# Moving the latent products of a pair of heads behind the transposes of the same slot

## The chip, the cores and the metric

The kernel runs on one core of a Trainium2 chip. The metric is the device time of one execution in microseconds (us), the median over the runs of a kernel. All times in the profile come from one profiled execution.

## The reference

Four sequences of 512 rows of width 512 pass through half a feed-forward step with low-rank adapters, an attention with a compressed key and value, and the feed-forward step again. The change lies in the attention alone:

```python
x = x + 0.5 * _L0_ffn_ref(_layernorm(x), ...)
x = x + _L0_attn_ref(_layernorm(x), ...)
x = x + 0.5 * _L0_ffn_ref(_layernorm(x), ...)

# _L0_attn_ref, H = 32 heads, latent width KVL = 64
q_lat = jnp.einsum('bhsd,hdr->bhsr', q_nope, wuk)
scores = jnp.einsum('bhsr,btr->bhst', q_lat, c_kv) + jnp.einsum('bhsd,btd->bhst', q_rope, k_rope[:, 0])
scores = scores / jnp.sqrt(jnp.float32(DN + DR))
scores = jnp.where(causal, scores, jnp.finfo(scores.dtype).min)
probs = jax.nn.softmax(scores, axis=-1)
out_lat = jnp.einsum('bhst,btr->bhsr', probs, c_kv)      # the latent products
out = jnp.einsum('bhsr,hdr->bhsd', out_lat, wuv)
return out.transpose(0, 2, 1, 3).reshape(b, s, H * DV) @ w_out
```

## The kernel before

The program is written engine by engine: each engine has its own queue with the order written out by hand, and semaphores tie them together. After an opening that loads and folds the weights, a loop runs three times and its body stands once more behind it for the fourth sequence: `attend(b)` (the attention of one sequence) and `steps(b, ...)` (the feed-forward steps and the projections for the next). In the loop a wait is on a value that is computed into a register first; in the copy for the fourth sequence waits are on constants.

`attend` goes over 16 pairs of heads. A pair has five units (`UNITS`), each one 128x512 bank of scores or less: the rows of a head with four key blocks (units 0 and 1, one for each head), with three and one (units 2 and 3), and the two-block rows of both heads (unit 4). So there are 80 slots, `u = 5*p + k`, and each engine walks through them with `work(g, u)`. In slot u:

- TensorE (PE) computes the scores of unit u (L849 to L851), in slots k = 0 and 2 the query products of the next pair (L834), the transposes of the probabilities of unit u - 3 (`T_LAG`; L870, four of 128x128), and in slots k = 1 and 4 an output product (L911, six matmuls) of heads two pairs or more back, from the fourth pair on. In slot k = 3 (`PV_SLOT`), the fourth of a pair, it also computes the latent products of the pair before, `pv(b, g, p - 1)` (L885, 20 entries in the trace).
- VectorE (DVE) adds the mask and takes the row minimum of the negated scores (L1490), the reciprocal of the row sums of the unit before (L1445), the rotary products of the queries (L1436 to L1438), the low part of the latent output (L1497), the copies of transposed units k = 1 and 3 (L369), and the output's addition to x (L1449).
- ScalarE (ACT) takes the exponentials with their row sums (L1120), the high parts of queries (L1091) and latent output (L1102), and the copies of transposed units k = 0, 2 and 4 out of PSUM into `probT` (L367).
- GpSimd (POOL) sums the rotary halves (L496), takes the low part of queries (L501) and multiplies the probabilities by the reciprocal sums (L576), one or two instructions for each unit.

What the slot k = 3 waits for. The transposes of unit 0 (`transpose_probs(b, g, u - 3)`) wait for POOL's multiplication of that unit (`prob_scaled`) and for the copy that frees their bank (`probT_by_dve`, the copy of unit 3 of the pair before). `pv` of the pair before waits for all copies of that pair: the last is ACT's copy of its unit 4 (`probT_by_act`), whose transposes stand in slot k = 2 and whose place on ACT is behind the exponentials of slot k = 2. It waits further for the two halves of the latent output before it (`oT_hi_set`, `oT_lo_set`). `probT` has one buffer, so the copies of the new pair wait for `pv_done`: ACT's copy of unit 0 stands in its slot k = 3 and waits for `pv_done` and for the transposes of unit 0. The scores of slot k = 4 follow on PE.

Of the kernel before, what the change touches and what calls it, by code (L numbers as in the profile page):

```python
# [72 lines left out]
T_LAG = 3  # L73
# [34 lines left out]
def build(nc, hidden, w_q_down, w_q_up_nope, w_q_up_rope, w_kv_down, w_k_rope, w_uk, w_uv, w_out,  # L108
          W_base, b_base, lora_A, lora_B, router_W, router_b, domain_prior, active,
          rope_cos, rope_sin, rope_cosT, rope_sinT, out):  # L110
    with ExitStack() as ctx:
# [206 lines left out]
        def attention(slot_work, tail):  # L318

            for g in range(BODIES):  # L320
                for u in range(BODY + (tail if g == BODIES - 1 else 0)):
                    slot_work(g, u)

        def known(g, u, least):

            return not isinstance(g, int) or BODY * g + u >= least

        def within(g, u, most):

            return not isinstance(g, int) or BODY * g + u <= most  # L330
# [5 lines left out]
        def output_rows(u):  # L336

            p, k = u // UNITS, u % UNITS
            slots = OUT_SLOT if u < BODY else OUT_SLOT_TAIL
            return 2 * ((p + 1) % 2) + slots[k] if k in slots else None  # L340
# [33 lines left out]
        def q_index(b, n, head):  # L374

            return 34 * b + 2 + 2 * n + head

        SLOTS = UNITS * PAIRS
        LAST_PAIR = PAIRS - 1

        with nc.Block() as block:
# [208 lines left out]
            def _(pe):  # L590
# [234 lines left out]
                def q_products(m, n, head, cols=slice(0, S), bank_free=True):  # L825

                    if bank_free:
                        pe.wait_ge(q_rot_set, m - 1)
                    hi, lo, rest = (w[:, 2 * n + head, :]
                                    for w in (wq1_hi, wq1_lo, wq2))  # L830
                    parts = ((hi, cq_hi[:, 0, cols]), (lo, cq_hi[:, 0, cols]), (hi, cq_lo[:, 0, cols]),
                             (rest, cq_hi[:, 1, cols]), (rest, cq_lo[:, 1, cols]))
                    for j, (w, c) in enumerate(parts):
                        last = nc.tensor.matmul(qT_ps[head][:, cols], w, c, start=(j == 0), stop=(j == 4))  # L834
                    last.then_inc(q_done, 1)

                def scores(b, g, u):
                    n = 80 * b + BODY * g + u
                    if u % UNITS < 2:
                        pe.wait_ge(qT_lo_set, q_index(b, BODY_PAIRS * g + u // UNITS, u % UNITS) + 1)  # L840
                    if known(g, u, 2):
                        pe.wait_ge(prob_set, n - 1)
                    par = (u // UNITS) % 2
                    members = [(c, (i + 1) * P, qT_hi[par][:, h, i * P:(i + 1) * P], qT_lo[par][:, h, i * P:(i + 1) * P])
                               for h, i, c in MEMBERS[u % UNITS]]
                    bank = score_ps[u % 2]

                    for c, w, high, low in members:
                        nc.tensor.matmul(bank[:, c:c + w], high, kT_hi[:, 0:w], start=True, stop=False)  # L849
                        nc.tensor.matmul(bank[:, c:c + w], high, kT_lo[:, 0:w], start=False, stop=False)  # L850
                        last = nc.tensor.matmul(bank[:, c:c + w], low, kT_hi[:, 0:w], start=False, stop=True)  # L851
                    last.then_inc(scores_ps, 1)

                def bank_copies(b, g, v):

                    pair = 16 * b + BODY_PAIRS * g + v // UNITS
                    return 3 * pair + ACT_COPIES[v % UNITS], 2 * pair + DVE_COPIES[v % UNITS]

                def transpose_probs(b, g, v):
                    pe.wait_ge(prob_scaled, 80 * b + BODY * g + v + 1)  # L860
                    if known(g, v, 2):
                        by_act, by_dve = bank_copies(b, g, v - 2)
                        if (v - 2) % UNITS in ACT_BANKS:
                            pe.wait_ge(probT_by_act, by_act)
                        else:
                            pe.wait_ge(probT_by_dve, by_dve)
                    for h, i, c in MEMBERS[v % UNITS]:
                        for j in range(i + 1):
                            at = slice(c + j * P, c + (j + 1) * P)
                            last = nc.tensor.transpose(probT_ps[v % 2][:, at], prob[v % RING][:, at], ident[:])  # L870
                    last.then_inc(probT_done, 1)

                def pv(b, g, p):

                    pair = 16 * b + BODY_PAIRS * g + p
                    by_act, by_dve = bank_copies(b, g, UNITS * p + UNITS - 1)
                    pe.wait_ge(probT_by_act, by_act)
                    pe.wait_ge(probT_by_dve, by_dve)
                    if known(g, UNITS * p, UNITS):
                        pe.wait_ge(oT_hi_set, pair)  # L880
                        pe.wait_ge(oT_lo_set, pair)
                    runs = ((0, 0, 3, 0), (0, 10, 1, 3), (1, 3, 3, 0), (2, 6, 2, 0), (3, 9, 1, 0))
                    for j, at, n, column in runs:
                        for h in range(2):
                            last = nc.tensor.matmul(o_ps[64 * h:64 * h + 64, column * P:(column + n) * P], ckv[:, j, :],  # L885
                                                    probT[:, HEAD_BLOCKS * h + at:HEAD_BLOCKS * h + at + n, :]
                                                    .rearrange("p s q -> p (s q)"), start=(j == 0 and column == 0),
                                                    stop=(j == 3 or column == 3), tile_position=(0, 64 * h),
                                                    skip_group_check=True)
                    last.then_inc(pv_done, 1)  # L890

                def output(b, g, p, t):

                    two = output_group(g, p)
                    first_pair = 2 * output_group(0, p)
                    n = 32 * b + 4 * two + t
                    if t == 0:
                        pe.wait_ge(oT_hi_set, 16 * b + 2 * two + 2)
                        pe.wait_ge(oT_lo_set, 16 * b + 2 * two + 2)
                    if not (isinstance(two, int) and two == 0 and t == 0):  # L900
                        pe.wait_ge(y_added, n)
                    for k in range(2):
                        last = output_products(two, oT_buffer(first_pair + k), t, k, out_ps)
                    last.then_inc(y_ps, 1)
# [10 lines left out]
                def last_outputs(b):  # L915

                    two = PAIRS // 2 - 1
                    pe.wait_ge(y_added, 32 * b + 4 * two)
                    pe.wait_ge(oT_hi_set, 16 * b + PAIRS - 1)
                    pe.wait_ge(oT_lo_set, 16 * b + PAIRS - 1)  # L920
                    for t in range(ST - 1):
                        output_products(two, oT_buffer(PAIRS - 2), t, 0, last_out_ps[t])
                    pe.wait_ge(oT_hi_set, 16 * b + PAIRS)
                    pe.wait_ge(oT_lo_set, 16 * b + PAIRS)
                    for t in range(ST):
                        if t == ST - 1:
                            output_products(two, oT_buffer(PAIRS - 2), t, 0, last_out_ps[t])
                        output_products(two, oT_buffer(PAIRS - 1), t, 1, last_out_ps[t]).then_inc(y_ps, 1)

                def attend(b):  # L930
                    def work(g, u):
                        k, p = u % UNITS, u // UNITS
                        if within(g, u, SLOTS - 1):
                            scores(b, g, u)
                        queries = within(g, u, UNITS * LAST_PAIR - 1)
                        n = BODY_PAIRS * g + p + 1
                        if k in (0, 2) and queries:
                            q_products(q_index(b, n, k // 2), n, k // 2)
                        if k == PV_SLOT and known(g, u, UNITS):
                            pv(b, g, p - 1)  # L940
                        if known(g, u, T_LAG) and within(g, u, SLOTS - 1 + T_LAG):
                            transpose_probs(b, g, u - T_LAG)
                        if output_rows(u) is not None and known(g, u, 3 * UNITS):
                            output(b, g, p, output_rows(u))
                    attention(work, TAIL)
                    last_outputs(b)
# [592 lines left out]
```

## Time and profile before

| | us |
|---|---|
| median of 3 runs | 1274.99 |
| lowest and highest | 1270.4, 1275.39 |
| the profiled execution | 1273.67 |
| its span, first to last instruction | 1271.8 |

| engine | busy us | share of the span |
|---|---|---|
| PE matmul | 1132.7 | 89% |
| DVE | 935.7 | 74% |
| POOL | 740.3 | 58% |
| ACT | 597.7 | 47% |

A line L885 is line 885 of the kernel. PE's ends are modelled, since matmuls are pipelined: the start of a row and the start of the next tell more than its length. "Idle" is the time in which an engine stood still before an instruction, with the instruction that ended the wait; "issue" there is a wait for nothing that the profile shows. In the chain of work that ended last each piece is followed back to what released it.

### The profile page before, as it was taken

To read this page: it belongs to the slowest core of one execution; us is meant where nothing else is said; L and a number is where in the kernel's file an instruction comes from. 1 tells how busy PE (TensorE), PEld (TensorE's weight loads), DVE (VectorE), ACT (ScalarE), POOL (GpSimd) and SP (SyncE) were. 2 spreads that over 40 slices of the span, in tenths; PEclk is the share of its full clock that TensorE was granted. 3 is DMA by queue.
4 is the path that set the end of the run, shared out by engine and by line. 5 is a ranking of instruction groups with operands and counts; after the bars stand their busy time and mean duration, and the time that the engine had idled before them with its cause. 6 is when DMAs were issued, how large, how long until landed. Compare 5 with 4: busy or idle time off the path is not lost.

```text
span 1271.8 us, 24129 instructions
## 1 busy us (share of the span) xinstructions
PE 1132.7 (89%) x7312; PEld 935.6 (74%) x7312; DVE 935.7 (74%) x3049; ACT 597.7 (47%) x1698; POOL 740.3 (58%) x943
## 2 busy tenths in 40 slices
PE   5978899999897899999887889999989689999996
PEld 4646777777695777777686677777769567777776
DVE  4767778886676877887667777788667668878855
ACT  3645555555133555555323455555512355555541
POOL 1417877776214877777303777777721387777741
PEclk9999999999898999999989999999989899999998
DMA  9740000000100000000100000000000000000000
GB/s 264 204 137 1 2 1 1 2 1 2 33 34 2 2 1 1 2 1 1 35 34 2 1 2 1 1 1 1 1 34 34 2 1 1 2 1 1 1 1 34
DMA packets 21674, 28.00 MB, mean 22 GB/s; under 512 B 10247, under 2 KB 12039, under 8 KB 20907
## 3 DMA queue, kind: packets, MB, share of 16 engines
q1 hardware_dynamic: 19178, 21.71, 5.5%
q10 hardware_dynamic: 2368, 4.72, 1.2%
q8 instruction: 65, 1.06, 0.4%
q14 instruction: 63, 0.51, 0.1%
HBM read 22.23 MB, written 4.19 MB: 21 GB/s over the span
## 4 chain that ended last, share of the span: by engine, by line
PE 50%; DVE 20%; issue 16%; ACT 6%; POOL 5%; SPq 1%; DMA 1%; DVEq 0%; ACTq 0%; POOLq 0%
PE Y L885 10%; PE Y L911 9%; PE XZ L870 6%; PE Y L616 5%; PE XZ L616 4%; PE Y L834 3%; DVE XZ L1490 3%; DVE q_turned L1437 3%; ACT prob L1120 3%; DVE q_sums L1436 3%; DVE probT L369 2%; PE XZ L849 2%; ACT probT L367 2%; PE XZ L851 2%; PE XZ L850 2%
## 5 line engine op out<-in xcount | busy, mean ns | idle before, releaser
L1120 ACT ACTIVATE prob<-XZ,small 128x512 f32<-128x512 f32 (+3 forms) x512 | 266.5, 525 | 344.3 <-DVE small L1490 343.9
L576 POOL TENSOR_TENSOR prob<-prob,small 128x512 f32<-128x512 f32 (+3 forms) x512 | 360.3, 721 | 63.6 <-DVE small L1445 47.1
L1490 DVE CUSTOM_DVE_ANT_0 XZ<-XZ,mask 128x512 f32<-128x512 f32 (+3 forms) x512 | 245.1, 510 | 162.3 <-issue 160.0
L496 POOL TENSOR_TENSOR q_sums<-q_sums,q_turned 64x512 f32<-64x512 f32 (+2 forms) x136 | 165.2, 1215 | 163.4 <-DVE q_turned L1438 159.6
L501 POOL TENSOR_TENSOR qT_lo<-q_sums,qT_hi 128x512 fp32r<-128x512 f32 (+2 forms) x136 | 166.0, 1221 | 79.6 <-ACT qT_hi L1091 79.6
L870 PE MATMUL XZ<-ident,prob 128*128 128x128 f32 x1280 | 196.0, 276 | 5.1 <-POOL prob L576 4.8
L885 PE MATMUL Y<-probT,ckv 128*64 128x384 f32 (+2 forms) x1280 | 155.6, 390 | 48.0 <-ACT probT L367 48.0
L849 PE MATMUL XZ<-kT_hi,qT_hi 128*128 128x512 f32 (+3 forms) x512 | 178.5, 349 | 17.3 <-POOL qT_lo L501 11.2
L870 PEld LDWEIGHTS XZ<-ident,prob 128*128 128x128 f32 x1280 | 150.2, 140 | 44.1 <-issue 14.4
L885 PEld LDWEIGHTS Y<-probT,ckv 128*64 128x64 f32 x1280 | 92.1, 139 | 105.6 <-issue 62.9
L850 PE MATMUL XZ<-kT_lo,qT_hi 128*128 128x512 f32 (+3 forms) x512 | 166.9, 326 | 0.0
L851 PE MATMUL XZ<-kT_hi,qT_lo 128*128 128x512 f32 (+3 forms) x512 | 166.7, 326 | 0.0
L367 ACT ACTIVATE probT<-XZ 128x512 f32<-128x512 f32 x192 | 114.6, 597 | 63.2 <-PE XZ L870 62.3
L849 PEld LDWEIGHTS XZ<-kT_hi,qT_hi 128*128 128x128 f32 x512 | 98.1, 192 | 27.6 <-ACT prob L1120 11.3
L1449 DVE TENSOR_TENSOR x_sb<-Y,x_sb 128x512 f32<-128x512 f32 x128 | 88.0, 687 | 35.1 <-PE Y L911 34.3
L911 PE MATMUL Y<-wo_hi,oT_hi 128*128 128x512 f32 x256 | 110.9, 433 | 1.6 <-DVE x_sb L1449 1.4
L470 POOL TENSOR_TENSOR var_eps<-moments,small 128x1 f32<-128x1 f32 (+3 forms) x26 | 5.2, 201 | 176.7 <-DVE moments L1152 176.7
L850 PEld LDWEIGHTS XZ<-kT_lo,qT_hi 128*128 128x128 f32 x512 | 98.7, 193 | 5.0
L851 PEld LDWEIGHTS XZ<-kT_hi,qT_lo 128*128 128x128 f32 x512 | 98.1, 192 | 5.7
L1120 ACT ACTIVATION_READ_ACCUMULATOR prob<-XZ,small 128x1 f32 x512 | 100.8, 197 | 1.0 <-issue 1.0
L911 PE MATMUL Y<-wo_hi,oT_lo 128*128 128x512 f32 x256 | 101.0, 395 | 0.0
L911 PE MATMUL Y<-wo_lo,oT_hi 128*128 128x512 f32 x256 | 100.3, 392 | 0.0
(199 smaller groups left out, 2300.2 us busy)
## 6 DMA issues: line engine op xcount, KB each, us to landing
wout_nat<-in_L_attn_w_out_dram SPq DMA_DIRECT2D x16, 512.0 KB, 4.3
out_dram<-x_sb SPq DMA_DIRECT2D x16, 256.0 KB, 2.0
x_next<-_attn_hidden_states_dram SPq DMA_DIRECT2D x12, 256.0 KB, 3.6
wbase_nat<-in_L_ffn_W_base_dram ACTq DMA_DIRECT2D x1, 1024.0 KB, 5.4
x_sb<-_attn_hidden_states_dram ACTq DMA_DIRECT2D x4, 256.0 KB, 6.8
nope_a<-_L_attn_w_q_up_nope_dram ACTq DMA_DIRECT2D x1, 1024.0 KB, 7.0
rope_a<-_L_attn_w_q_up_rope_dram SPq DMA_DIRECT2D x1, 1024.0 KB, 8.8
rope_bb<-_L_attn_w_q_up_rope_dram SPq DMA_DIRECT2D x2, 512.0 KB, 11.4
```

Source lines behind the costliest of these rows:

```text
L367: do.activation(probT_unit(v), bank_unit(v), ACT.Copy).then_inc(probT_by_act, 1)
L496: nc.gpsimd.tensor_tensor(q, q, turned, ALU.add).then_inc(q_sum_set, 1)
L501: nc.gpsimd.tensor_tensor(qT_lo[par][:, head, cols], q_sums[par][:, head, cols], f32(qT_hi[par][:, head, cols]), ALU.subtract).then_inc(qT ...
L576: last = nc.gpsimd.tensor_tensor(prob[u % RING][:, c:c + w], prob[u % RING][:, c:c + w], inv_sum[:, u % RING, m:m + 1].broadcast_to([P, w] ...
L849: nc.tensor.matmul(bank[:, c:c + w], high, kT_hi[:, 0:w], start=True, stop=False)
L850: nc.tensor.matmul(bank[:, c:c + w], high, kT_lo[:, 0:w], start=False, stop=False)
L851: last = nc.tensor.matmul(bank[:, c:c + w], low, kT_hi[:, 0:w], start=False, stop=True)
L870: last = nc.tensor.transpose(probT_ps[v % 2][:, at], prob[v % RING][:, at], ident[:])
L885: last = nc.tensor.matmul(o_ps[64 * h:64 * h + 64, column * P:(column + n) * P], ckv[:, j, :], probT[:, HEAD_BLOCKS * h + at:HEAD_BLOCKS * ...
L911: last = nc.tensor.matmul(bank, o[buffer][:, rows], w, start=(k == 0 and j == 0), stop=(k == 1 and j == 2))
L1120: last = nc.scalar.activation(prob[u % RING][:, c:c + w], score_ps[u % 2][:, c:c + w], ACT.Exp, bias=neg_max[:, u % RING, m:m + 1], scale= ...
L1490: last = nc.vector.tensor_tensor_reduce(bank, bank, mask[:, S - w:S], -1.0, HIGHEST, ALU.add, ALU.min, neg_max[:, u % RING, m:m + 1])
```

## The change

In PE's walk through the slots, the transposes of a slot now come before the latent products where both stand in one slot, k = 3. Nothing else in the source is touched, and the queues of DVE, ACT, POOL and SyncE are the same.

```diff
                         if k in (0, 2) and queries:
                             q_products(q_index(b, n, k // 2), n, k // 2)
+                        if known(g, u, T_LAG) and within(g, u, SLOTS - 1 + T_LAG):
+                            transpose_probs(b, g, u - T_LAG)
                         if k == PV_SLOT and known(g, u, UNITS):
                             pv(b, g, p - 1)
-                        if known(g, u, T_LAG) and within(g, u, SLOTS - 1 + T_LAG):
-                            transpose_probs(b, g, u - T_LAG)
                         if output_rows(u) is not None and known(g, u, 3 * UNITS):
                             output(b, g, p, output_rows(u))
```

A sequence has 16 `pv`: 15 share their slot with transposes, the last (slot 83) has none beside it and stays where it is. So 60 of 64 are touched.

PE's queue in the loop, slot k = 3 of a pair, from the last score matmuls to the latent products, before. `REGISTER_ALU` computes the value for a wait; what stands in brackets is what an entry waits for:

```order
L850 MATMUL XZ<-kT_lo,qT_hi_126 128x128
L851 MATMUL XZ<-kT_hi,qT_lo_128 128x128
L877 REGISTER_ALU
L878 REGISTER_ALU [waits probT_by_act]
L885 MATMUL Y<-probT,ckv 64x384 [waits oT_lo_set,oT_hi_set,probT_by_dve]
L885 MATMUL Y<-probT,ckv 64x384
L885 MATMUL Y<-probT,ckv 64x128 x2
L885 MATMUL Y<-probT,ckv 64x384 x2
L885 MATMUL Y<-probT,ckv 64x256 x2
L885 MATMUL Y<-probT,ckv 64x128 x2
L870 MATMUL XZ<-ident,prob_105 128x128 [waits probT_by_dve,prob_scaled]
L870 MATMUL XZ<-ident,prob_105 128x128 x3
```

The same place in the changed kernel:

```order
L866 REGISTER_ALU [waits prob_scaled]
L870 MATMUL XZ<-ident,prob_105 128x128 [waits probT_by_dve]
L870 MATMUL XZ<-ident,prob_105 128x128 x3
L877 REGISTER_ALU
L885 MATMUL Y<-probT,ckv 64x384 [waits oT_hi_set,oT_lo_set,probT_by_dve,probT_by_act]
L885 MATMUL Y<-probT,ckv 64x384
L885 MATMUL Y<-probT,ckv 64x128 x2
L885 MATMUL Y<-probT,ckv 64x384 x2
L885 MATMUL Y<-probT,ckv 64x256 x2
L885 MATMUL Y<-probT,ckv 64x128 x2
```

The four transposes moved from behind the latent products to ahead of them, and the register computation that waited for ACT's copy is gone: the wait for `probT_by_act` now stands last in the list of the first latent product itself.

PE's queue in the copy for the fourth sequence, where waits are on constants, before:

```order
L885 MATMUL Y<-probT,ckv 64x384 [waits oT_hi_set,oT_lo_set,probT_by_dve,probT_by_act]
L885 MATMUL Y<-probT,ckv 64x384
L885 MATMUL Y<-probT,ckv 64x128 x2
L885 MATMUL Y<-probT,ckv 64x384 x2
L885 MATMUL Y<-probT,ckv 64x256 x2
L885 MATMUL Y<-probT,ckv 64x128 x2
L870 MATMUL XZ<-ident,prob_104 128x128 [waits probT_by_dve,prob_scaled]
L870 MATMUL XZ<-ident,prob_104 128x128 x3
```

Here the first latent product had that list of waits already; in the changed kernel the two transposing entries stand ahead of it and its list is the same.

## Rows read from the trace of the kernel before

**Rows 1.** The page: engines' busy time (parts 1), and the chain by engine.

```profile
PE 1132.7 (89%) x7312; PEld 935.6 (74%) x7312; DVE 935.7 (74%) x3049; ACT 597.7 (47%) x1698; POOL 740.3 (58%) x943
...
PE 50%; DVE 20%; issue 16%; ACT 6%; POOL 5%; SPq 1%; DMA 1%; DVEq 0%; ACTq 0%; POOLq 0%
```

**Rows 2.** Waits: engine, line, what it waited for, us in total, times, longest.

```profile
PE Y L885 <- ACT probT L367: 48.0, 60, 1.8
```

**Rows 3.** Timeline, PE, a pair of the third sequence: start, us, what [idle before].

```profile
863.16 0.27 PE L851 MATMUL XZ<-kT_hi,qT_lo 128*128 128x128 f32 x1
864.13 2.38 PE L885 MATMUL Y<-probT,ckv 128*64 128x384 f32 x20 [0.70 <-ACT probT L367]
866.44 0.66 PE L870 MATMUL XZ<-ident,prob 128*128 128x128 f32 x4
866.85 0.36 PE L849 MATMUL XZ<-kT_hi,qT_hi 128*128 128x256 f32 x1
...
878.40 0.55 PE L885 MATMUL Y<-probT,ckv 128*64 128x384 f32 x2 [0.70 <-ACT probT L367]
```

**Rows 4.** Timeline, ACT, the same pair: its copies of unit 4 and unit 0.

```profile
863.30 0.59 ACT L367 ACTIVATE probT<-XZ 128x512 f32<-128x512 f32 x1
...
867.21 0.60 ACT L367 ACTIVATE probT<-XZ 128x512 f32<-128x512 f32 x1 [0.79 <-PE XZ L870]
```

**Rows 5.** Chain that ended last, the same pair: start, us, what.

```profile
863.90 0.23 issue
864.13 2.38 PE Y L885 x20
866.51 0.59 PE XZ L870 x4
...
878.17 0.23 issue
```

**Rows 6.** Timeline, DVE, the same pair: its two waits.

```profile
867.86 0.43 DVE L1490 CUSTOM_DVE_ANT_0 XZ<-XZ,mask 128x256 f32<-128x256 f32 x1 [2.47 <-issue]
...
869.68 0.69 DVE L1449 TENSOR_TENSOR x_sb<-Y,x_sb 128x512 f32<-128x512 f32 x1 [0.34 <-PE Y L911]
```

**Rows 7.** Timeline, POOL, the same pair: query sum and the scalings of units 0, 1.

```profile
859.55 1.30 POOL L496 TENSOR_TENSOR q_sums<-q_sums,q_turned 64x512 f32<-64x512 f32 x1 [1.41 <-DVE q_turned L1438]
861.01 1.04 POOL L576 TENSOR_TENSOR prob<-prob,small 128x512 f32<-128x512 f32 x1 [0.16 <-POOL q_sums L496]
...
863.25 1.04 POOL L576 TENSOR_TENSOR prob<-prob,small 128x512 f32<-128x512 f32 x1
```

**Rows 8.** Timeline, PE, a pair of the fourth sequence.

```profile
1111.56 0.27 PE L851 MATMUL XZ<-kT_hi,qT_lo 128*128 128x128 f32 x1
1112.35 2.38 PE L885 MATMUL Y<-probT,ckv 128*64 128x384 f32 x20 [0.51 <-ACT probT L367]
1114.66 0.66 PE L870 MATMUL XZ<-ident,prob 128*128 128x128 f32 x4
```

**Rows 9.** Timeline, ACT, that pair: the copy of unit 4.

```profile
1111.70 0.59 ACT L367 ACTIVATE probT<-XZ 128x512 f32<-128x512 f32 x1
```

**Rows 10.** Timeline, ACT and PE, second sequence, copy of unit 4 and first latent products.

```profile
418.27 0.59 ACT L367 ACTIVATE probT<-XZ 128x512 f32<-128x512 f32 x1
...
418.99 2.38 PE L885 MATMUL Y<-probT,ckv 128*64 128x384 f32 x20 [0.77 <-ACT probT L367]
```

**Rows 11.** Timeline, POOL and PE, third sequence: scaling of unit 0, first latent products.

```profile
719.86 1.04 POOL L576 TENSOR_TENSOR prob<-prob,small 128x512 f32<-128x512 f32 x1 [0.16 <-DVE small L1445]
...
721.89 2.38 PE L885 MATMUL Y<-probT,ckv 128*64 128x384 f32 x20 [0.74 <-ACT probT L367]
```

**Rows 12.** Busy time by window: us, PE, PEld, DVE, ACT, POOL, granted clock, DMA.

```profile
735.30:738.70 3.40, 3.40 (x20) 1.98 (x15) 0.77 (x5) 1.02 (x4) 2.69 (x4) 0.51 0.00 0
```

**Rows 13.** Timeline, PE, latent products in that window.

```profile
734.82 4.06 PE L885 MATMUL Y<-probT,ckv 128*64 128x384 f32 x20 [1.23 <-ACT probT L367]
```

**Rows 14.** Busy time of L885 alone by window, first sequence: us, PE, PEld, clock.

```profile
94.00:328.00 234.00, 38.08 (x320) 23.35 (x320) 0.99 0.02 6
```

## The prediction

> **What bounds the kernel now.** I read the page first: PE is busy for 89% of the span and holds half of the chain that ended last, DVE a fifth of it [rows 1]. Neither engine alone is the bound, so I looked for the places where the two hand over. The list of waits has one on PE that stands out: the latent products (L885) wait for ACT's copy of transposed probabilities (L367), 60 times for 48.0 us together [rows 2]. A sequence has 320 entries of L885, that is 16 groups of 20 [rows 14], so 64 groups in all, and nearly each of them waits.
>
> Then I followed one pair of heads through the timelines. On PE the last score matmul of slot 3 starts at 863.16, the latent products start at 864.13 after 0.70 us of idle time, the four transposes follow at 866.44 and the scores of slot 4 at 866.85; the next pair's latent products start at 878.40, 14.27 us after the first [rows 3]. On ACT the copy that is waited for ends at 863.30 + 0.59 = 863.89 [rows 4]. On DVE there are two waits in the pair: 2.47 us until 867.86, when it begins on the scores of slot 4, and 0.34 us for an output product [rows 6]. Outside these two DVE works without a pause from the first scores of the next pair up to its copy and minima, and ACT's next copy of unit 4 hangs on these minima. So the period of a pair is one loop: latent products, transposes, scores, output product and scores on PE, then DVE's stretch, then ACT's exponentials and copy, then latent products again. The chain says the same: in a pair it has 0.23 us of "issue" ahead of L885, 2.38 us of L885 and 0.59 us of transposes, and comes back to the same 0.23 us one period later [rows 5]. Whatever is cut between the end of ACT's copy and the scores of slot 4 shortens the period, as long as nothing outside that loop is as long.
>
> **The change part by part.**
>
> *The transposes leave the loop.* They are taken from behind the latent products, where they hold back slot 4 by 866.85 - 866.44 = 0.41 us [rows 3], and go into the idle time ahead. Do they fit? PE can take the next entry about 0.11 us after the start of the last score matmul, at 863.27 (a matmul of 128 columns; in the same rows the transposes' own starts are that far apart, 0.41 us for four). Behind them PE is free at about 863.68, before the copy's end at 863.89 [rows 3, 4]. So they cost nothing there and save 0.41 us. In the fourth sequence the idle time is 0.51 us, and the copy ends at 1111.70 + 0.59 = 1112.29; the transposes would be through at about 1111.56 + 0.11 + 0.41 = 1112.08 [rows 8, 9]. They fit as well.
>
> Are their operands there? They need POOL's scaling of unit 0, which is the one behind the sum of the first head's query halves: it ends at 861.01 + 1.04 = 862.05, over 1.2 us before PE could begin [rows 7]. In the first pair of a sequence, where the margin is least, it ends at 719.86 + 1.04 = 720.90, while the latent products start at 721.89 [rows 11]: with 0.41 us for the transposes there is 0.5 us of margin still. The bank that they write was copied by DVE in the slot before, as the wait inside the latent products demands in any case.
>
> Count: 15 of 16 groups in each sequence have transposes beside them, 60 in all. 60 x 0.41 = 24.6 us. Bounds: 0.59 us if the scores of slot 4 had to wait for the transposes' ends, as the chain counts it [rows 5], and 0.33 us if they cost only three steps of 0.11 us; 60 times that is 20 to 35 us. I take 0.41 us, because it is start to start at this very place. That products hand over to scores as fast as to transposes isn't in the trace; the transposes start 0.07 us ahead of the products' modelled end.
>
> *The wait for ACT's copy gets shorter in the loop.* Before, the wait stands on a register computation (L878), and behind it come the waits for the latent halves and the first product. From the end of the copy to the first product the trace has 864.13 - 863.89 = 0.24 us [rows 3, 4]. In the fourth sequence the wait for the copy stands on the first product itself, last in its list, and there it is 1112.35 - 1112.29 = 0.06 us [rows 8, 9]. In the changed kernel the looped product has the same list in the same order. So I take 0.24 - 0.06 = 0.18 us for each looped pair. The first pair of a sequence has no latent halves to wait for, and there it is 418.99 - 418.86 = 0.13 us now [rows 10], so 0.07 us. Bounds: 0 if the register computation that is left (L877) or the waits are worked off only behind the copy, 0.18 if as in the fourth sequence. The idle time allows it: from 863.68 to 863.95 PE is still waiting. Sum: 42 x 0.18 + 3 x 0.07 = 7.8 us. The fourth sequence gains nothing by this.
>
> *What is later.* Nothing on other queues is moved. ACT's copy of unit 0 waits for both transposes and products; it starts at 867.21 now, 0.79 us after ACT had nothing to do [rows 4], and will hang on the products alone, so it comes 0.4 us or more earlier. SyncE, with its loads of the next sequence, is far from this path. What comes next as the bound is PE itself: a period of 14.27 - 0.41 - 0.18 = 13.68 us leaves some 0.27 us of waiting before the latent products. In the fourth sequence the pair has the same form and loses its 0.41 us.
>
> *Sum.* 24.6 + 7.8 = 32.4 us. Against the profiled execution: 1273.67 - 32.4 = 1241.3 us. The median of the runs shown is 1.3 us above that execution and would give 1242.6; I forecast **1242 us**.
>
> *The clock.* In the second pair of the third sequence the granted clock was 0.51 over 3.4 us, the lower of its two levels (1.2 and 2.4 GHz), and the products took 4.06 us instead of 2.38, so 1.68 us more; ahead of it PE had stood idle for 1.23 us [rows 12, 13, 3]. The other sequences pass that pair at full clock, so this falls or doesn't fall by how the work happens to lie. I take no change, and 1.7 us either way for each such place. The Trainium skill ("TensorE: Matmul & The Clock Gate", Part 4) says that a transpose on PE does not count as busy for the clock in the way a matmul does. By that rule the transposes in the gap would not keep the clock up, and such falls stay as frequent as now; no row here separates transposes from matmuls in this respect. By the opposite reading the fall would go, and the sum would be 34.1 us.
>
> **The rivals.**
>
> 1. *Only the transposes count.* The first product's waits turn out to be worked off behind the copy also in the new order, so the 0.24 us stays. For: the value for the wait on the copy still comes from a register in the loop, unlike in the fourth sequence. Against: the computation no longer waits for the copy itself, and PE stands idle with time for it. 1273.67 - 24.6 = 1249 us.
>
> 2. *The clock gives part back.* PE's gaps of the early pairs move against each other, and the clock falls in the second pair in all four sequences instead of one: 3 x 1.68 = 5 us more than the forecast, 1247 us. For: the longest gap of such a pair is only filled in part, and one fall is there already. Against: three of four sequences have the same gap today and keep the clock.
>
> 3. *Nothing, or nearly nothing, comes of it*, because the loop that I read isn't what sets the period, and DVE's 2.47 us of waiting, which the profile puts down to "issue" [rows 6], end for some other reason than the scores of slot 4. For: DVE is on the chain with 20% [rows 1]. Against: the wait ends right behind PE's scores of slot 4. 1268 to 1274 us.
>
> 4. *Slower.* The transposes wait for POOL, and everything behind PE's queue waits with them. It needs the scaling of unit 0 to be late: if it were the one that starts at 863.25 and ends at 864.29 [rows 7], the transposes would begin at about 864.4, and the products at 864.8 instead of 864.13. The pair would lose 0.67 us and win back 0.41: 60 x 0.26 = 16 us, 1289 us. It decides from the point where the scaling ends later than about 863.5, and it ends 1.5 us before that if I have told the two scalings apart. The order on POOL (sum of the first head's halves, scaling of unit 0, low part, scaling of unit 1) speaks against it.
>
> **How the numbers follow.** Forecast (both parts) 0.67, rival 1 0.18, rival 2 0.06, rival 3 0.05, rival 4 0.04. The range reaches from the forecast with both of the short clock falls gone and a base as low as the lowest run (1242 - 3.4 - 2.6 = 1236) up to rival 1 with two clock falls more (1252). What lies outside is rivals 3 and 4 and the edges, about 1 in 8. A measurement of this kernel can tell about 0.5% from no change, 6.4 us: the forecast and rivals 1 and 2 are faster by more, 0.91 and a part of rival 3, so 0.92; 0.04 for within it, 0.04 for slower.
>
> **What would show it.** In the profile of the changed kernel the timeline should have the transposes right behind the scores of slot 3, then some 0.3 us of waiting by starts, then the latent products 0.06 us after ACT's copy ends, in looped sequences too, and the scores of slot 4 directly behind the products. The period of a pair should be 13.68 us in the loop and 0.41 us shorter than now in the fourth sequence. The waits of PE for L367 should fall from 48 us to below 20. The forecast is wrong if the transposes are found waiting for POOL, if the 0.24 us is still there, or if the waiting reappears before another entry of PE while the period stays at 14.27.

## The result and the profile after

| | before | after |
|---|---|---|
| median, us | 1274.08 | 1239.34 |
| lowest and highest, us | 1270.4, 1275.39 | 1238.8, 1240.14 |
| the profiled execution, us | 1273.67 | 1239.81 |
| its span, us | 1271.8 | 1238.0 |

The ratio of after to before is 0.9732, with a 95% interval of 0.971 to 0.9755. The change makes the kernel 2.7% faster.

On PE, a pair of the third sequence, the one behind that of [rows 3]:

```profile
853.36 0.28 PE L851 MATMUL XZ<-kT_hi,qT_lo 128*128 128x128 f32 x1
853.47 0.62 PE L870 MATMUL XZ<-ident,prob 128*128 128x128 f32 x4
854.15 2.38 PE L885 MATMUL Y<-probT,ckv 128*64 128x384 f32 x20
856.46 0.39 PE L849 MATMUL XZ<-kT_hi,qT_hi 128*128 128x256 f32 x1
...
867.84 2.38 PE L885 MATMUL Y<-probT,ckv 128*64 128x384 f32 x20
```

The transposes start 0.11 us after the last score matmul, without a wait, and the scores of slot 4 start 2.31 us after the products, where the transposes used to start. From one group of products to the next it is 867.84 - 854.15 = 13.69 us; it was 14.27.

On ACT, the copies of unit 4 and of unit 0, as in [rows 4]:

```profile
853.50 0.60 ACT L367 ACTIVATE probT<-XZ 128x512 f32<-128x512 f32 x1
...
856.58 0.60 ACT L367 ACTIVATE probT<-XZ 128x512 f32<-128x512 f32 x1
```

The copy of unit 4 ends at 854.10 and the products start at 854.15: 0.05 us instead of 0.24. The copy of unit 0 no longer waits for the transposes.

The chain that ended last, in that pair, as in [rows 5]:

```profile
853.61 0.50 ACT probT L367
854.11 0.04 issue
```

Its 0.23 us of "issue" have become 0.04, and ACT's copy is still what releases the products. PE still waits for it, then, and is not yet the bound.

On POOL, the sum of the query halves and the scaling of unit 0 of the next pair, as in [rows 7]:

```profile
863.44 1.29 POOL L496 TENSOR_TENSOR q_sums<-q_sums,q_turned 64x512 f32<-64x512 f32 x1 [1.41 <-DVE q_turned L1438]
864.89 1.04 POOL L576 TENSOR_TENSOR prob<-prob,small 128x512 f32<-128x512 f32 x1 [0.16 <-POOL q_sums L496]
```

It ends at 865.93, and PE takes its transposes up at 867.16, 1.23 us later. In the first two pairs of a sequence the transposes have no such margin. PE and POOL in the first pair of the third sequence:

```profile
704.72 0.28 PE L851 MATMUL XZ<-kT_hi,qT_lo 128*128 128x128 f32 x1
704.89 0.65 PE L870 MATMUL XZ<-ident,prob 128*128 128x128 f32 x4
705.68 2.38 PE L885 MATMUL Y<-probT,ckv 128*64 128x384 f32 x20
```

```profile
703.72 1.04 POOL L576 TENSOR_TENSOR prob<-prob,small 128x512 f32<-128x512 f32 x1 [0.16 <-DVE small L1445]
```

The scaling ends at 704.76 and the transposes start 0.13 us later. They are 0.17 us behind the last score matmul instead of 0.11, so for a moment they do wait for POOL. It costs nothing, since ACT's copy, at 705.62, ends later still.

The waits for ACT's copy, as in [rows 2]:

```profile
PEld Y L885 <- ACT probT L367: 26.6, 60, 1.7
PE Y L885 <- ACT probT L367: 9.6, 13, 1.5
```

The 48.0 us of PE have fallen to 9.6. That count leaves out the short waits: in the pair above the transposes' modelled end, 853.47 + 0.62 = 854.09, reaches up to the products. The loads of the weights for the same products still stand before this wait 60 times.

In the fourth sequence, where waits are on constants, PE and ACT, as in [rows 8, 9]:

```profile
1094.92 0.62 PE L870 MATMUL XZ<-ident,prob 128*128 128x128 f32 x4
1095.60 2.38 PE L885 MATMUL Y<-probT,ckv 128*64 128x384 f32 x20
```

```profile
1094.95 0.59 ACT L367 ACTIVATE probT<-XZ 128x512 f32<-128x512 f32 x1
```

The copy ends at 1095.54 and the products start 0.06 us later, as before. The period is 13.69 us here too; it was 14.08.

**Where the time came from.** From the first group of products of a sequence to its last the trace of before has 206.77, 206.78, 208.45 and 205.57 us, and that of after 198.29, 198.35, 198.26 and 198.06. The difference is 34.6 us in sum; the rest of the span grew by 0.8 us, which makes 33.8. Of the 34.6 us, 3.3 are two stretches at the lower clock that are gone. One is that of [rows 12, 13], 1.68 us. The other is in the first products of the fourth sequence, which took 4.01 us before and 2.38 after. In the second pair of the third sequence the granted clock is now 1.00:

```profile
717.00:721.00 4.00, 3.46 (x29) 2.19 (x29) 2.38 (x9) 2.49 (x11) 3.68 (x4) 1.00 0.01 4
```

What is left for the change itself is 31.3 us: 0.58 us a pair in the loop and 0.39 us in the fourth sequence.

### The profile page after: what moved, and what is told of

Read it like the earlier page. It is cut to its first block, busy times and chain, and to the rows that moved or that the text cites. A ratio compares the mean times of both kernels' runs of the same rounds, so it can differ in the third digit from the quotient of the medians.

```text
span 1238.0 us, 24129 instructions
## 1 busy us (share of the span) xinstructions
PE 1133.4 (92%) x7312; PEld 922.9 (75%) x7312; DVE 935.7 (76%) x3049; ACT 596.1 (48%) x1698; POOL 740.3 (60%) x943
## 4 chain that ended last, share of the span: by engine, by line
PE 49%; DVE 21%; issue 15%; ACT 7%; POOL 5%; SPq 1%; DMA 1%; DVEq 0%; ACTq 0%; POOLq 0%
PE Y L885 11%; PE Y L911 10%; PE Y L616 5%; PE XZ L616 4%; PE XZ L870 4%; DVE XZ L1490 4%; PE Y L834 4%; DVE q_turned L1437 3%; PE XZ L849 3%; ACT prob L1120 3%; DVE q_sums L1436 3%; DVE probT L369 2%; ACT probT L367 2%; PE XZ L851 2%; PE XZ L850 2%
## 5 line engine op out<-in xcount | busy, mean ns | idle before, releaser
L870 PEld LDWEIGHTS XZ<-ident,prob 128*128 128x128 f32 x1280 | 150.1, 140 | 33.8 <-POOL prob L576 6.3
L885 PE MATMUL Y<-probT,ckv 128*64 128x384 f32 (+2 forms) x1280 | 152.3, 384 | 12.3 <-ACT probT L367 9.6
L885 PEld LDWEIGHTS Y<-probT,ckv 128*64 128x64 f32 x1280 | 81.8, 136 | 83.1 <-issue 47.2
```

## The experiments

Each ratio below is to executions of the kernel before that were taken beside the run; their median was 1274.08 us for runs 1 to 4, 1274.54 for runs 5 to 8 and 1275.31 for run 9. "Period" is the distance between the starts of two neighbouring groups of latent products from the fourth pair of a sequence on, where it repeats.

### 1. The shorter wait alone

```diff
 def pv(b, g, p):
-    pe.wait_ge(probT_by_act, by_act)
-    pe.wait_ge(probT_by_dve, by_dve)
     if known(g, UNITS * p, UNITS):
         pe.wait_ge(oT_hi_set, pair)
         pe.wait_ge(oT_lo_set, pair)
+    pe.wait_ge(probT_by_dve, by_dve)
+    pe.wait_ge(probT_by_act, by_act)
```

This is the kernel before with only these lines changed.

> The kernel before, with the order of work untouched; only the waits of the latent products stand in another order, the one for ACT's copy last and on the first product itself, behind all register computations. Theory (two terms that add up): the 0.24 us from the copy's end to the products becomes 0.06 us in the loop, the period of a pair falls from 14.27 to 14.09 us there, and the fourth sequence stays at 14.08. Sum 42 x 0.18 + 3 x 0.07 = 7.8 us, so about 1266 us beside 1274. Rival (the shorter wait comes only with the transposes ahead of it, because PE works the waits off while it transposes): no change, 1274 us and 0.24 us still there.

Measured: 1267.25 us, ratio 0.9955 (0.994 to 0.997), so 6.8 us less. Its timelines of ACT and PE:

```profile
855.98 0.59 ACT L367 ACTIVATE probT<-XZ 128x512 f32<-128x512 f32 x1
```

```profile
856.62 1.73 PE L885 MATMUL Y<-probT,ckv 128*64 128x384 f32 x12 [0.51 <-ACT probT L367]
```

The copy ends at 856.57 and the products start 0.05 us later. The period in the loop is 14.08 us, as expected, and from the first to the last group of products each looped sequence takes 2.6 us less (the third, where a stretch at the lower clock is gone besides, 4.3): three times 2.6 are the 7.8 us. That the whole gained less comes from the fourth sequence. It was to stay as it was and took 1.3 us more, with a period of 14.17 us in place of 14.08. ACT and PE there:

```profile
1174.77 0.59 ACT L367 ACTIVATE probT<-XZ 128x512 f32<-128x512 f32 x1
```

```profile
1175.51 2.38 PE L885 MATMUL Y<-probT,ckv 128*64 128x384 f32 x20 [0.61 <-ACT probT L367]
```

The products start 0.14 us after the copy's end there, where the kernel before has 0.05. In that kernel's queue on constants the wait for ACT, first in the source, stands last in the list. If the order is turned round here too, it now stands first; no view of this run's queue shows it. The second term of the prediction is an effect of its own: it can be had in the loop without moving any work.

### 2. The transposes alone

```diff
 def pv(b, g, p):
     pe.wait_ge(probT_by_act, by_act)
+    pe.wait_ge(scores_ps, (45 + 2 * (BODY_PAIRS * g + p)) * b + 1)
     pe.wait_ge(probT_by_dve, by_dve)
```

This is the changed kernel with one more wait, which is always satisfied by then. It is there to put a register computation behind the wait for ACT again.

> The changed kernel, with one more wait in the latent products, on a count that was reached long ago and whose value needs a register of its own, so that a register computation stands behind the wait for ACT's copy again, as it did before the change. Theory: only the transposes' term is left, 60 x 0.41 = 24.6 us, so the period in the loop is 13.87 us instead of 13.69 and the time about 1247 to 1248 us; the fourth sequence stays at 13.69. Rival (the transposes' move alone bought all of it): 1239 us.

Measured: 1254.27 us, ratio 0.9847 (0.9831 to 0.9864). ACT and PE:

```profile
866.72 0.59 ACT L367 ACTIVATE probT<-XZ 128x512 f32<-128x512 f32 x1
```

```profile
867.66 0.54 PE L886 MATMUL Y<-probT,ckv 128*64 128x384 f32 x2 [0.35 <-ACT probT L367]
```

It is 15 us slower than the changed kernel, not 8. From the copy's end at 867.31 to the products it is 0.35 us: by the source four other waits stand behind the one for the copy, where before the change there were three and it took 0.24. The period is 13.99 us in the loop, where 13.87 was expected: 0.30 more than 13.69, and 0.35 - 0.05 is just that. The fourth sequence stays at 13.69 us, as expected. The 0.11 us by which this wait is longer than that of before, in 45 pairs, are 5 us; without them the kernel would be 24.8 us faster than before (1274.08 - 1254.27 + 5.0). That is the transposes' term by the medians, predicted at 24.6. By the periods it is 14.27 - 13.99 + 0.11 = 0.39 us a pair, and 60 x 0.39 = 23.4 us; the medians may hold some gain of clock besides, since both of the stretches at the lower clock in the pairs of before are gone in this run's trace too. So the term is 23 to 25 us. The rival, that the move of the transposes alone bought everything, is out.

### 3 to 5. How late POOL may be

```diff
 # POOL, work(g, u), ahead of the scaling of the unit; twice in runs 4 and 5
+if k == 0:
+    nc.gpsimd.tensor_tensor(scratch[:], mask[:], mask[:], ALU.mult)
```

Where it stands twice, the second waits for the first. Run 5 has the same two in the kernel before.

> The changed kernel with one needless multiplication of 128x512 on POOL ahead of the scaling of unit 0, about 1.3 us. In the trace of the changed kernel that scaling ends 1.2 us before PE begins the transposes, and behind them PE waits 0.3 us more. Theory (POOL has that margin and no more): scaling of unit 0 ends about when PE wants it, 1239 to 1242 us. Rival (POOL is already near the path through the low part of the queries, which is pushed back too): each pair loses up to 1.3 us, 1260 us or more.

> The changed kernel with two such multiplications on POOL, about 2.7 us with the wait between them. Theory (the margin of 1.2 + 0.3 us is overrun): PE stands at the transposes, and the latent products and all behind them wait for POOL; each of 60 pairs loses about 1.2 us, 1310 us. Rival (the transposes' place doesn't matter to POOL): 1239 us.

> The kernel before with the two needless multiplications on POOL that the changed kernel had in the run e4_pool_late_twice (1303 us, period 14.53 us). Theory (with the transposes behind the products, POOL's scaling of unit 0 may be some 3 us later before anyone waits): the period stays at 14.27 us; outside the pairs the multiplications cost what they cost in e4, about 64 - 60 x 0.84 = 14 us, so about 1288 us, and with a POOL as late as this the change would make the kernel slower by about 15 us. Rival (POOL's lateness costs the same in either order): about 1274 + 64 = 1338 us.

Measured: 1248.01 us with one (0.9803, 0.9784 to 0.9822), 1303.31 with two (1.0226, 1.0209 to 1.0243), and 1285.31 for the kernel before with two (1.0086, 1.0068 to 1.0104).

With one, the period is 13.69 us as in the changed kernel. Behind the same products the scaling of unit 0 ends 12.71 us later instead of 11.78, so the pairs paid nothing for 0.9 us of lateness, and 0.31 us are left from its end to the transposes where there were 1.23. The time missed my range of 1239 to 1242 all the same. The 8.5 us by which its span is longer stand elsewhere: 3.0 us before the first products, 3.1 us between sequences, 1.3 us in one single pair of 15.02 us, and 0.3 us in each second pair. I hadn't thought of these places. At least a part of it is PE waiting for POOL where the changed kernel has no margin, as in the second pair of the third sequence, here with the products 0.38 us behind the copy's end instead of 0.05:

```profile
724.66 0.65 PE L879 MATMUL XZ<-ident,prob 128*128 128x128 f32 x4 [0.79 <-POOL prob L585]
```

With two, PE and POOL in the changed order:

```profile
858.36 0.65 PE L879 MATMUL XZ<-ident,prob 128*128 128x128 f32 x4 [0.79 <-POOL prob L585]
858.94 2.38 PE L894 MATMUL Y<-probT,ckv 128*64 128x384 f32 x20
```

```profile
855.07 2.16 POOL L577 TENSOR_TENSOR scratch<-mask 128x512 f32<-128x512 f32 x2
857.19 1.04 POOL L585 TENSOR_TENSOR prob<-prob,small 128x512 f32<-128x512 f32 x1
```

PE stands at the transposes until the scaling of unit 0 ends at 858.23, with the products behind it. From the products before it that end is 13.82 us away instead of 11.78, so it is 2.0 us late. The period is 14.53 us, 0.84 more than 13.69: 1.2 us of the lateness are margin, and the rest is paid. I had expected 1.2 us a pair and 1310 us, with 2.7 us of lateness and 1.5 of margin; the two multiplications took 2.16 us. The same two multiplications with the products ahead of the transposes, PE:

```profile
871.63 2.38 PE L894 MATMUL Y<-probT,ckv 128*64 128x384 f32 x20 [0.69 <-ACT probT L369]
873.94 0.66 PE L879 MATMUL XZ<-ident,prob 128*128 128x128 f32 x4
```

Here the scaling ends at 871.58 and nobody asks for it until 873.94; the period is 14.26 us, as without them. So with a POOL that is this late the change would have made the kernel slower, by 18 us (1303.31 - 1285.31). In the pairs that is 0.27 us in the loop and 0.44 in the fourth sequence; about 4 us more of the profiled executions are three stretches at the lower clock, which the pairs of run 4 have and those of run 5 don't. That is rival 4 of the prediction. Its point of decision lay 1.2 us behind the scaling's end, where I had put 1.5.

### 6. ACT's copy ahead of the exponentials, in the changed kernel

```diff
 # ACT, work(g, u)
+v = u - T_LAG
+copies = (known(g, u, T_LAG) and within(g, u, SLOTS - 1 + T_LAG)
+          and v % UNITS in ACT_BANKS)
+if copies and k == 2:
+    copy_probT(act, nc.scalar, b, g, v)
 if within(g, u, SLOTS - 1):
     ...                                  # the exponentials of unit u
-v = u - T_LAG
-if known(g, u, T_LAG) and within(g, u, SLOTS - 1 + T_LAG) and v % UNITS in ACT_BANKS:
+if copies and k != 2:
     copy_probT(act, nc.scalar, b, g, v)
```

> The changed kernel with ACT's copy of unit 4 ahead of the exponentials of its slot instead of behind them; the order on PE, DVE and POOL is the same. Theory (the 0.27 us that PE still waits for that copy is all that stands between the pair and PE's own pace): the copy comes 0.9 us earlier, the period falls from 13.69 to about 13.42 us, and the time to 1223 to 1226 us. Rival (the exponentials of unit 2 come 0.6 us later, and DVE's reciprocal, POOL's scaling and the scores behind them wait for that): no gain or a loss, 1239 us or more.

Measured: 1224.24 us, ratio 0.9609 (0.9589 to 0.9629), 15 us below the changed kernel. ACT and PE:

```profile
857.79 0.60 ACT L367 ACTIVATE probT<-XZ 128x512 f32<-128x512 f32 x1 [0.97 <-PE XZ L870]
```

```profile
858.29 0.28 PE L851 MATMUL XZ<-kT_hi,qT_lo 128*128 128x128 f32 x1
858.40 0.62 PE L870 MATMUL XZ<-ident,prob 128*128 128x128 f32 x4
858.95 2.38 PE L885 MATMUL Y<-probT,ckv 128*64 128x384 f32 x20
861.26 0.39 PE L849 MATMUL XZ<-kT_hi,qT_hi 128*128 128x256 f32 x1
```

The copy ends at 858.39, before the transposes even start. PE now waits for nobody in the pair. Yet the period is 13.58 us and not 13.42: from the transposes to the products it is 0.55 us, where I had counted 0.41. So the time came out in my range partly by luck. Of the 15 us the repeating pairs give 0.11 us each, about 5 us. More comes from the first two distances between products in each sequence and the one before the last, which I hadn't counted apart: there the changed kernel still waited longer for the copy, and they shrank by some 0.6, 0.4 to 0.5 and 0.85 us, nearly 8 us in all.

### 7. Two transposes ahead, two behind

```diff
 # transpose_probs(b, g, v, part): part 0 takes two of the four blocks, part 1 the others
-transpose_probs(b, g, u - T_LAG)
+both = k == PV_SLOT and known(g, u, UNITS)
+transpose_probs(b, g, u - T_LAG, 0 if both else None)
 if k == PV_SLOT and known(g, u, UNITS):
     pv(b, g, p - 1)
+    if within(g, u, SLOTS - 1 + T_LAG):
+        transpose_probs(b, g, u - T_LAG, 1)
```

> The changed kernel with two of the four transposes of the slot ahead of the latent products and two behind. Theory (what counts is PE's time behind the products): half of the 0.41 us comes back into the period, 13.69 + 0.2 = 13.9 us, and the time is about 1251 us. Rival (what counts is that ACT's copy of unit 0 hangs on the products alone): the whole 0.41 us comes back, 1264 us.

Measured: 1250.51 us, ratio 0.9811 (0.9794 to 0.9829), period 13.87 us. PE:

```profile
874.98 0.41 PE L872 MATMUL XZ<-ident,prob 128*128 128x128 f32 x2
875.66 2.38 PE L888 MATMUL Y<-probT,ckv 128*64 128x384 f32 x20 [0.27 <-ACT probT L367]
877.97 0.44 PE L872 MATMUL XZ<-ident,prob 128*128 128x128 f32 x2
```

Half of the transposes behind the products cost 0.18 us of period, nearly half of 0.41. ACT's copy of unit 0 hangs on the transposes again here, and that didn't bring the whole amount back. What counts is the time that PE spends behind the products.

### 8 and 9. The old order without the wait

Run 8 has the edit of run 6 in the kernel before. Run 9 has that of run 1 in addition.

> The kernel before with ACT's copy of unit 4 ahead of the exponentials of its slot. Theory (the change pays only because PE stood idle for that copy): without that wait the order of transposes and products makes no difference, so this is as fast as e6_copy_first within 0.5%, about 1225 us, with a period near 13.42 us. Rival (the order itself is worth 0.4 us a pair, as through ACT's copy of unit 0): 20 us or more slower than e6.

> The kernel before (latent products ahead of the transposes) with ACT's copy of unit 4 ahead of the exponentials and, in the latent products, the wait for that copy last and on the first product. In e8_before_copy_first the period was 13.63 us in the loop, where the products still started 0.24 us after the copy's end, and 13.49 in the fourth sequence; in e6_copy_first, with the transposes ahead, 13.58 in both. Theory (transposes handing over to latent products cost PE some 0.09 us a pair more than the old order, which shows once PE waits for nobody): 13.49 us in the loop too, 42 x 0.14 = 6 us below e8, about 1220 us, and 4 us below e6. Rival (the 0.14 us in e8 isn't the wait's form): no change from e8, 1225 us.

Measured: 1225.55 us for run 8 (0.9613, 0.9596 to 0.963) and 1220.71 for run 9 (0.9575, 0.9559 to 0.9591). Run 8's period is 13.63 us in the loop and 13.49 in the fourth sequence, where 13.42 was expected. ACT and PE, in the loop:

```profile
859.23 0.60 ACT L367 ACTIVATE probT<-XZ 128x512 f32<-128x512 f32 x1 [0.97 <-PE XZ L870]
```

```profile
859.73 0.27 PE L851 MATMUL XZ<-kT_hi,qT_lo 128*128 128x128 f32 x1
860.07 1.41 PE L885 MATMUL Y<-probT,ckv 128*64 128x384 f32 x10
```

Run 9, PE, in the loop:

```profile
867.81 0.27 PE L851 MATMUL XZ<-kT_hi,qT_lo 128*128 128x128 f32 x1
868.01 2.38 PE L885 MATMUL Y<-probT,ckv 128*64 128x384 f32 x20
870.32 0.66 PE L870 MATMUL XZ<-ident,prob 128*128 128x128 f32 x4
870.73 0.36 PE L849 MATMUL XZ<-kT_hi,qT_hi 128*128 128x256 f32 x1
```

This is the strictest test of the theory. In their source run 8 and run 6 differ only in the order that this case is about, and in time by 1.3 us; run 8 has the longer form of the wait besides. So the order as such is worth nothing; all of the transposes' 0.41 us came from a gap that ACT's copy had left on PE. In run 8 the products still start 0.24 us after the copy's end at 859.83, and run 9 takes that away: 868.01 - 867.81 = 0.20 us from the last score matmul to the products instead of 0.34, and a period of 13.49 us instead of 13.63. From that score matmul to the scores of slot 4 run 9 needs 870.73 - 867.81 = 2.92 us and run 6, with the transposes ahead, 861.26 - 858.29 = 2.97. With the same short wait the new order is even the slower one, by 0.09 us a pair. The time of run 9 is 4.8 us below run 8 and 3.5 below run 6, where 6 and 4 were expected: the looped sequences gave 1.9 to 2.1 us each, but the fourth took 0.5 us more, with 13.53 us instead of 13.49 and, as in run 1, 0.14 us from the copy's end to the products. Run 9 is the fastest kernel of this case, 18.6 us below the changed kernel by the medians, and it has the old order.

## Why the prediction was right

It said 1242 us, and 1239.34 was measured. By its own steps:

*What bounds the kernel.* The loop over PE, DVE and ACT was read rightly, and what was cut between ACT's copy and the scores of slot 4 came out of the period: 0.58 us of the 0.59 that I counted. Rival 3, that DVE's waits end for another reason, is out: its wait before the scores of slot 4 fell from 2.47 us to 1.90, and the period with it.

```profile
857.48 0.43 DVE L1490 CUSTOM_DVE_ANT_0 XZ<-XZ,mask 128x256 f32<-128x256 f32 x1 [1.90 <-issue]
```

*The transposes.* 24.6 us predicted; run 2, corrected for its longer wait, gives 24.8 by the medians and 23.4 by the periods, and the fourth sequence, where nothing else changed, 0.39 us a pair instead of 0.41. I had left open whether the products hand over to scores as fast as to transposes; they do, 2.31 us after the products' start in either case. POOL's operands were there 1.2 us early from the fourth pair on, as said, but not in the first two pairs. In the first pair I had found 0.5 us of margin before the products would be held up. The transposes started as soon as POOL was through and the products 0.79 us later, where run 6 needs 0.58, so 0.2 us were left.

*The shorter wait.* 7.8 us predicted from the fourth sequence's form of the same wait. The loop of run 1 gained 0.19 us a pair (14.27 to 14.08) and 7.8 us in all; its median, with the loss in the fourth sequence, 6.8. Rival 1 is out.

*The period.* 13.68 us predicted, 13.69 measured, in the fourth sequence too. In sum the change itself gave 31.3 us instead of 32.4. Of the missing 1.1 us, 0.2 are the 3 x 0.07 us of the first pairs, which lie ahead of the first products and so outside these distances. The rest is 0.39 us a pair instead of 0.41 in the fourth sequence and 0.58 instead of 0.59 in the loop.

*What is next.* I gave 0.27 us to PE's waiting; PE's own pace in this order turned out to be 13.58 us (run 6), so only 0.11 us were left. The one step that was mis-sized is the price of the transposes in their new place: I took 0.41 us for them ahead of the products as behind, and ahead it is 0.55. Of the 0.14 us more, 0.09 are the products' own: they start 0.20 us behind a score matmul too (run 9), where I had taken 0.11 for whatever comes next. It cost nothing in the result, since it lay in the gap. It is also why the margin in rival 4 was 1.2 us and not 1.5.

*The clock.* I took no change; two stretches at the lower clock went, 3.3 us in all, and that is what brings the span's 33.8 us above my 32.4. I had priced one of them beside the forecast and both in the range. If the other executions lost these 3.3 us too, the median without that is 1242.6 us, 0.6 from the forecast. The Trainium skill ("TensorE: Matmul & The Clock Gate", Part 4) says that transposes don't count as busy like matmuls, and by that rule the falls should have stayed. They went, in the one profile of the changed kernel, but run 1 has a fall in the fourth sequence with the old gap and none in the third, where before had one, run 5 has none in its pairs with the old gap, and run 4 has three with the new order. These runs don't tell a cause from chance, and the question stays open.

*Slower.* Rival 4 could happen, and runs 4 and 5 made it happen, with 1.2 us of margin instead of 1.5.

## What to carry to other kernels

When an engine waits for a copy at one entry of its queue and ready work stands right behind that entry, move the work ahead of it: it pays the length of the work as far as the gap reaches, and it costs the whole lateness of that work's own operands as soon as they aren't early. Then ask why the gap is there, since the order that hides a gap is worth nothing once the gap is closed; here moving one copy on ACT bought 49 us (run 8), and the reordering on PE 35. And let the wait that ends last stand last, on the instruction itself: a register computation behind it is paid after it. Measure it in each copy of the code: the order in the source that won 0.19 us a pair in the loop lost 0.09 in the copy on constants (run 1).

## What the runs showed of the hardware

- In the loop the same wait on PE cost 0.05 us when it stood on the product itself (0.05 to 0.06 in the fourth sequence), 0.24 us when a register computation carried it and the other waits came behind it, and 0.35 us with one wait more behind it (run 2). That PE works such entries off during a wait only if they stand ahead of it fits runs 1, 2, 8 and 9. In the fourth sequence of runs 1 and 9 it cost 0.14 us, with the waits in the other order in the source and all on constants. The Trainium skill ("Perfetto Trace Analysis", Identifying Dependency Chains) says that an instruction that waits for several engines may get extra instructions for the further waits ahead of it; in the loop before it was a register computation that carried one of the four.
- Four 128x128 transposes took 0.41 us start to start when score matmuls followed and 0.55 us when products on 64 columns followed (run 6). In those 0.55 us the last transpose starts 0.35 us after the first, and the products 0.20 us after that; behind the last score matmul the products took 0.20 us too (run 9), where transposes took 0.11. Why the products start later behind either is not settled.
- The lower clock came and went between kernels that differ in fractions of a microsecond per pair; the two stretches in the pairs of before cost 1.68 and 1.63 us (products in 4.06 and 4.01 us instead of 2.38).
